# Attention scores of three sequences in two single-pass parts, rows to the operand tile by way of DRAM, and a new instruction order

## The reference, cut to what matters

```python
x = x + _L0_attn_ref(_layernorm(x), ...)  # "s": convolution, then a scan over 512 steps of 256 x 16 states
x = x + _L0_ffn_ref(_layernorm(x), ...)   # "g": gated experts, 8 experts of which at most 2 count
x = x + _L1_attn_ref(_layernorm(x), ...)  # "t": attention, below
x = x + _L1_ffn_ref(_layernorm(x), ...)   # "f": ternary weights, 128 -> 512 -> 512 -> 512 -> 128
```

```python
def _L1_attn_ref(x, W_DQ, W_UQ, W_QR, W_DKV, W_UK, W_UV, W_KR, W_O):
    ...                                    # 16 heads, 8 plain and 4 rotated columns each
    Q = jnp.concatenate([Qc, Qr], axis=-1)
    K = jnp.concatenate([Kc, Kr], axis=-1)
    scores = jnp.einsum('bhqd,bhkd->bhqk', Q, K)
    scores = jnp.clip(scores, -80.0, 80.0)
    causal = jnp.tril(jnp.ones((S, S), dtype=bool))
    scores = jnp.where(causal, scores, -jnp.inf)
    weights = jax.nn.softmax(scores / jnp.sqrt(jnp.float32(d_qk)), axis=-1)
    attn = jnp.einsum('bhqk,bhkd->bhqd', weights, V)
```

## Time and profile before

| | before |
|---|---|
| time, median of 3 runs | 1694.17 us (1692.5 to 1697.28) |
| the profiled execution: its own time, its span | 1694.72 us, 1693.1 us |
| PE busy | 1541.0 us, 91% |
| DVE, ACT, POOL busy | 1393.5, 1257.4, 1136.6 us |

### The profile page before, as it was taken

How to read it: one execution, slowest core, us unless ns; L and a number is a source line. 1 busy time by engine, 2 the same in 40 slices (tenths; PEclk the granted TensorE clock), 3 DMA queues, 4 the chain that set the end, 5 groups by cost and what they waited for, 6 DMA issues and landing times. The chain is left out here.

```text
span 1693.1 us, 24277 instructions
## 1 busy us (share of the span) xinstructions
PE 1541.0 (91%) x7911; PEld 814.3 (48%) x7911; DVE 1393.5 (82%) x2695; ACT 1257.4 (74%) x2160; POOL 1136.6 (67%) x1019
## 2 busy tenths in 40 slices
PE   5446799999999999999999999999999799999997
PEld 2123344444444444444444434434444478788875
DVE  4899988999999999999999999997331677977773
ACT  4776788899898899989899898885656455555552
POOL 4996787878788887878888787885122255554442
PEclk9678799999999999999999999999999799999998
DMA  4000000000000000000000000002000000000000
GB/s 155 1 0 0 19 1 20 7 14 19 2 20 1 20 7 14 19 1 20 1 20 9 12 20 1 20 1 88 20 4 17 1 1 13 14 13 14 13 13 27
DMA packets 14689, 27.87 MB, mean 16 GB/s; under 512 B 3853, under 2 KB 4438, under 8 KB 14042
## 3 DMA queue, kind: packets, MB, share of 16 engines
q1 hardware_dynamic: 14554, 26.24, 5.4%
HBM read 9.46 MB, written 4.19 MB: 8 GB/s over the span
## 5 line engine op out<-in xcount | busy, mean ns | idle before, releaser
L615 POOL TENSOR_TENSOR sum_fast<-sum_fast,state_fast 128x512 f32<-128x512 f32 x448 | 578.0, 1290 | 74.1 <-DVE state_fast L597 41.0
L597 DVE TENSOR_TENSOR_SCAN state_fast<-state_fast,bank 128x512 f32<-128x512 f32 x512 | 597.9, 1199 | 8.8 <-ACT state_fast L582 7.9
L1007 ACT ACTIVATE prob_fast<-bank 128x1024 f32<-128x1024 f32 x320 | 325.0, 1017 | 117.4 <-PE bank L991 110.8
L991 PE MATMUL bank<-stacks_fast 64*128 64x512 f32 (+3 forms) x2048 | 363.6, 464 | 18.7 <-ACT prob_fast L1007 11.7
L582 ACT ACTIVATE state_fast<-chan_all_kept,neg_a_fast 128x512 f32<-128x512 f32 x512 | 349.7, 712 | 13.1 <-POOL sum_fast L615 7.4
L1051 POOL TENSOR_SCALAR_AFFINE_SELECT prob_fast<-prob_fast 128x512 f32<-128x512 f32 x256 | 165.6, 659 | 226.9 <-ACT prob_fast L1007 226.6
L991 PEld LDWEIGHTS bank<-stacks_fast 64*128 64x128 f32 x2048 | 171.6, 186 | 238.9 <-issue 101.1
L1643 POOL TENSOR_TENSOR cell_a_fast<-th_fast,cell_a_fast 128x512 fp32r<-128x512 f32 x64 | 90.1, 1408 | 154.9 <-ACT cell_a_fast L1518 154.9
L1068 PE MATMUL bank<-prob_fast,v_ext_fast 128*32 128x512 f32 (+3 forms) x2048 | 177.1, 441 | 15.9 <-POOL prob_fast L1051 8.1
L485 PE MATMUL bank<-xnt_s_fast,taps_fast 128*128 128x512 f32 (+3 forms) x256 | 129.7, 654 | 33.8 <-DVE chan_all_kept L540 22.8
L669 PE MATMUL bank<-resid_m_fast,xnt_g_fast 128*128 128x512 f32 x256 | 143.7, 646 | 10.4 <-DVE gate_fast L750 9.5
(11 more groups left out here) (205 smaller groups left out, 2497.5 us busy)
## 6 DMA issues: line engine op xcount, KB each, us to landing
stacks_fast<-parts_fast SPq DMA_DIRECT2D x128, 64.0 KB
stacks_fast<-rest_fast SPq DMA_DIRECT2D x128, 32.0 KB
out_x<-f_out_fast SPq DMA_DIRECT2D x16, 256.0 KB, 2.0
x_res_kept<-in_x SPq DMA_DIRECT2D x1, 2048.0 KB, 15.3
chan_all_kept<-in_h_t SPq DMA_DIRECT2D x2, 1024.0 KB, 7.3
x_res_kept<-in_x SPq DMA_DIRECT2D x1, 1024.0 KB, 10.9
chan_all_kept<-in_w_t SPq DMA_DIRECT2D x3, 256.0 KB, 2.9
x_res_kept<-in_x SPq DMA_DIRECT2D x2, 256.0 KB, 3.7
```

The source lines that it names most:

```text
L597: dve.tensor_tensor_scan(h[:], h[:], self.banks[0][:], 0.0, ALU.mult, ALU.add).then_inc(self.v_scan.sem)
L615: pool.tensor_tensor(total[:], total[:], h[:], ALU.add).then_inc(self.p_sum.sem)
L991: ins = pe.matmul(self.scores(b, step)[:, c:c + SEQ - P * kt], rows[:, 1, h // 2, P * kt:P * kt + P], rows[:, 0, h // 2, P * kt:SEQ], star ...
L1007: act.activation(self.probs[u % 2][:, i * 1024:(i + 1) * 1024], self.scores(b, 5 * g + n)[:], ACT.Exp, scale=SCALE).then_inc(self.a_prob.sem)
```

## The change

Line numbers in this section's rows of the new kernel are its own: L1055 is the score matmul (L991 before), L704 L669, L683 L648, L713 L678, L891 L854, L898 L859, L908 to L911 L869 to L872, L1132 L1068, L1139 L1075.

1. From sequence 13 on (`SPLIT = 13`), queries and keys are split into a part hi, rounded to the type fp32r, and the rest lo. hi and lo of a head's 12 rows stand below each other in `stacks`, keys as hi, lo, hi, lo and queries as hi, lo, lo, hi, so that 48 of the 64 rows hold all four products, and one matmul in fp32r takes the place of one in float32. ACT's copy rounds; DVE subtracts it from the PSUM bank (L965, 2 a sequence); POOL copies and subtracts the rotated rows (2 a sequence).
2. For every sequence, the rows go first to DRAM (`rows_q`, `rows_k`, two buffers each, taken in turn) and from there to `stacks`. Up to sequence 12 this takes 4 + 8 DMAs of 64 to 256 KB instead of 16 of 32 and 64 KB; from 13 on 10 + 16. `parts` and `rest0` are free when their rows are in DRAM, and no longer when `stacks` is written.
3. Small setup tiles share the room of `num`.
4. `TIMES` and `EDGES` are new: every engine's order in phase one changes.

```diff
-PERIOD, F_PERIOD = 70626, 24942
+PERIOD, F_PERIOD = 73747, 24942
...
-DMA_SIGNALS = {"stack_lo": 8, "stack_hi": 8}
+
+SPLIT = 13
+DMA_SIGNALS = {"out_rot": 2, "out_q": 1, "out_k": 1, "stack_lo": 4, "stack_hi": 4}
+DMA_SPLIT = {"out_rot_split": 5, "out_q_split": 3, "out_k_split": 2, "stack_lo_split": 8, "stack_hi_split": 8}
...
+        hi, lo = (self.rot_hi[:].bitcast(F32), self.rest[1]) if split else (self.rest[0], None)
+        for at, src in ((DH, hi), (DQK + DH, lo), (2 * DQK + DH, hi))[:3 if split else 1]:
+            sp.dma_start(q[s, at:at + DR].rearrange("d h p c -> (d h p) c"), src[0:NQ]).then_inc(out_rot.sem, 16)
...
+        for i, rows in enumerate((q, k)):
+            hi, lo = self.parts[:, i].bitcast(F32), self.parts_lo[:, i].bitcast(F32)
+            yield
+            sp.wait_ge(self.a_t_qk.sem, self.a_t_qk.at(b, i))
+            if split:
+                sp.wait_ge(self.v_t_lo.sem, self.v_t_lo.at(b - SPLIT, i))
+            for at, src in ((0, hi), (DQK, lo), (2 * DQK, hi))[:3 - i if split else 1]:
+                sp.dma_start(rows[s, at:at + DH].rearrange("d h p c -> (d h p) c"), src).then_inc(out_rows[i].sem, 16)
+        for half, name in enumerate(("stack_lo", "stack_hi")):
+            cols, moved = slice(half * PAIRS // 2, (half + 1) * PAIRS // 2), self.on_way(name, b)[0]
+            yield
             if b:
                 sp.wait_ge(self.t_score.sem, self.t_score.at(b - 1, 5 * GROUPS // 2 * (half + 1) - 1))
...
+            sp.wait_ge(out_rot.sem, self.on_way("out_rot", b)[1])
+            for i, rows in enumerate((q, k)):
+                sp.wait_ge(out_rows[i].sem, self.on_way("out_k" if i else "out_q", b)[1])
+                for parity in range(2):
+                    n = 2 * DQK if split else DQK
+                    for twice in range(2 if split else 1):
+                        r, at = 64 * parity + n * twice, 0 if i else DQK * twice
+                        sp.dma_start(stacks[r:r + n, i, cols].bitcast(F32),
+                                     rows[s, at:at + n, 2 * parity + half]).then_inc(moved.sem, 16)
...
         pe.wait_ge(self.a_t_sq.sem, self.a_t_sq.at(b, 1))
+        if b >= SPLIT:
+            pe.wait_ge(self.v_t_lo.sem, self.v_t_lo.at(b - SPLIT, 1))
...
+            dve.tensor_tensor(self.parts_lo[:, i], bank[:], parts[:, i].bitcast(F32), ALU.subtract).then_inc(self.v_t_lo.sem)
...
+        pool.tensor_copy(hi[:], full[:]).then_inc(done.sem)
+        pool.wait_ge(done.sem, done.at(b - SPLIT, 0))
+        pool.tensor_tensor(self.rest[1][:].bitcast(F32R), full[:], hi[:].bitcast(F32), ALU.subtract).then_inc(done.sem)
...
                     rows = stacks[64 * (h % 2):64 * (h % 2) + 64]
+                    rows = rows if b >= SPLIT else rows.bitcast(F32)
```

More of the change, by code:

```diff
@@ L886, in act_t_proj @@
             if b:
-                act.wait_ge(self.stack_lo.sem, self.stack_lo.at(b - 1, 7))
-                act.wait_ge(self.stack_hi.sem, self.stack_hi.at(b - 1, 7))
+                written, value = self.on_way("out_k" if i else "out_q", b - 1)
+                act.wait_ge(written.sem, value)
                 if i == 0 and not general:
                     act.wait_ge(self.t_t_norm.sem, self.t_t_norm.at(b - 1))
-            act.activation(parts[:, i], bank[:], ACT.Copy).then_inc(self.a_t_qk.sem)
+            act.activation(parts[:, i] if b >= SPLIT else parts[:, i].bitcast(F32), bank[:], ACT.Copy).then_inc(self.a_t_qk.sem)
             act.activation(self.squares[:, i], bank[:], ACT.Square).then_inc(self.a_t_sq.sem)
@@ L979, in pe_scores @@
                 if n == 0 and g % 2 == 0:
-                    moved = self.stack_hi if g else self.stack_lo
-                    pe.wait_ge(moved.sem, moved.at(b, 7))
+                    moved, value = self.on_way("stack_hi" if g else "stack_lo", b)
+                    pe.wait_ge(moved.sem, value)
                 step = 5 * g + n
@@ L1149, in act_t_setup @@
         act.wait_ge(self.t_fold_t.sem, self.t_fold_t.at(0, 0))
-        act.activation(self.lat_t[:], bank[0:2 * LAT, 0:DM], ACT.Copy)
+        act.activation(self.lat_t, bank[0:2 * LAT, 0:DM], ACT.Copy)
         for swap in range(2):
@@ L1227, in pe_t_setup @@
         pe.wait_ge(self.v_center.sem, self.v_center.at())
-        pe.matmul(bank[0:2 * LAT, 0:DM], self.lat_w[:], self.center[:], start=True, stop=True)
-        pe.matmul(bank[:, DM:DM + 2 * DR], self.center[:], self.kr_w[:], start=True, stop=True).then_inc(self.t_fold_t.sem)
+        pe.matmul(bank[0:2 * LAT, 0:DM], self.lat_w, self.center[:], start=True, stop=True)
+        pe.matmul(bank[:, DM:DM + 2 * DR], self.center[:], self.kr_w, start=True, stop=True).then_inc(self.t_fold_t.sem)
         yield
@@ L1242, in pool_setup @@
         pool.memset(self.eps[:], EPS).then_inc(self.p_eps.sem)
-        pool.memset(self.stacks[:], 0.0).then_inc(self.p_stacks.sem)
+        pool.memset(self.stacks[:].bitcast(F32), 0.0).then_inc(self.p_stacks.sem)
         for v in self.v_ext:
@@ L1814 @@
     t["out"] = nc.dram_tensor("out_x", (P, NSEQ * NT, DM), F32, kind="ExternalOutput").ap()
+    t["rows_q"] = nc.dram_tensor("rows_q", (2, 3 * DQK, 4, PAIRS // 2, SEQ), F32, kind="Internal").ap()
+    t["rows_k"] = nc.dram_tensor("rows_k", (2, 2 * DQK, 4, PAIRS // 2, SEQ), F32, kind="Internal").ap()
     build(nc, t)
```

272 lines of the change are left out of this document (148 added, 124 removed).

## The result

The changed kernel takes 1707.94 us, median of 4 runs (1706.2 to 1710.92), against 1694.54 for the kernel before on the same chip. The ratio is 1.0077, 95% interval 1.0063 to 1.0091: slower by 0.8%. I had forecast 1677, faster, with 1653 to 1695 as the range. The profiled execution has a span of 1709.4 us.

What follows compares the result with a forecast made beforehand. PE and DVE were taken to bound the middle, PE alone the stretch behind the last scan. 1172.1 + 48.9 + 43.1 + 4.5 + 22.5 + 9.3 = 1300.4 against 1317.9, 17.5 less, so 1677 us from 1694.2; range 1653 to 1695.

Steps and rivals of the forecast that it cites:

- The five marks of my sum: End of phase one: 13's scores at 1172.1, windows 48.9, 43.1, 4.5 waiting, 22.5 and 9.3 to the end: 1300.4.
- The price of a score step: Score matmuls from sequence 13 on: 0.40 us in fp32r against 1.06 in float32, 39.6 us saved over three sequences.
- I put the new order's effect on the middle at zero: Sequences 0 to 12: periods stay at 73.5 us, the longer DMA hop hidden behind 17 us of PE rows.
- the rival of the winning middle: The new order also fills PE's 1.9 us idle a period, up to 21 us: 1652 to 1668, chance 0.23.
- The slower rival, the gate in the middle: PE waits at L713 for the gate each period, 11 to 12 us per us lost; 1704 at 2.5; chance 0.13.
- y comes at about 1162: Behind the last scans: the last y at about 1162, PE waiting from 1153, scores of 13 at 1172.
- Sequences 13 and 14: Windows between first scores: 13 falls from 64.1 to 48.9 us, 14 from 56.5 to 43.1, the gate of 15 costing 3.
- The rows' way: Sequence 15's keys by DRAM to stacks: 13.0 us from the keys' start, PE waiting 4.5 us for the DMA.
- The rows' path makes the time: Rival: slow loads of 192 KB into stacks make each of three sequences wait 5 us more: 1692, chance 0.08.
- The clock: Rival: PE's clock falls to 0.5 in the last 32 us, costing 12 us: 1689, chance 0.11.
- one of my signs of being wrong: Signs: periods differing by 0.5 us or more, a PE wait at L713 in each, or clock 0.5 before 1290.

Runs made afterwards that it cites:

- the best: Changed kernel with twelve parts of sequences 12 to 15 moved and the projection making the keys' rotated rows 16 times (64 partitions): 1675.2 us, ratio 0.9889.
- the kernels with twelve and thirteen moves: Changed kernel with twelve or thirteen parts of sequences 12 to 15 moved in the engines' order: 1700.9 us with twelve, 1708.6 with thirteen.
- the old order: Changed kernel, split and way by DRAM kept, with the order tables of the kernel before: 1804.8 us, ratio 1.0657.
- the last four kernels: Changed kernel with rows from 64 partitions, 1703.0 us; with twelve moves, 1700.9; with both, 1675.2; with both and all scores in float32, 1700.1.
- the order without the way: Changed kernel with twelve parts of sequences 12 to 15 moved, the slow rows' way kept: 1700.9 us, ratio 1.0034.
- the way without the order: Changed kernel where the projection makes the keys' rotated rows 16 times, so DMAs read 64 partitions, nothing moved: 1703.0 us, ratio 1.0048.

## Why the prediction was wrong

The five marks of my sum against the trace: the last scan 1152.9 (measured 1137.5), scores of 13 at 1172.1 (1169.3), then 48.9 (65.8), 43.1 and 4.5 (62.4), and 31.8 to the end (37.2). So -15.4 to the last scan, +12.6 from there to the scores, +16.9, +14.8 and +5.4: 34.3 in all, 1334.7 for 1300.4. Of the 14.8, 2.0 are a slip of mine in adding: 56.5 - 13.2 - 2.8 + 1.6 + 3 is 45.1 and not 43.1, and the forecast should have read 1679.

Two steps made the forecast wrong: the waits behind the last scan, which I took over from the kernel before, and the price of the rows' way.

**The price of a score step was right** (0.43 us for 0.40). But 0.40 was a choice between bounds, and the weight loads that I worked it out from don't show: at full clock, steps of four matmuls take 0.44 us and steps of two 0.43. What it is worth wasn't: of 39.6 us, 15.8 in the changed kernel and 25 in the best (18 by its profiled execution). I had taken it off two windows as if PE stayed their limit. PE's work did go away; idle time and half clock stepped in.

**The middle**: "I put the new order's effect on the middle at zero" failed in my favour. It gives 1.0 us a period, as in the rival of the winning middle, which I gave 0.23. The slower rival, the gate in the middle, did not happen.

**"y comes at about 1162"**, 9 us behind the last scan: it came 17 behind (1154.6, where L683 starts), since POOL stood 4.7 us in front of sequence 13's rotated rows with the last scans' sums queued behind them. I had counted DVE's rows there and not POOL's.

**Sequences 13 and 14**: I counted what moved on PE and took over the waits of before. The order and the split's pieces made new ones. PE's values can't start before their shared bank has been read: in the new order they stand right behind the keys and wait 2.2 us for ACT's squares even without the split, and 2.9 with the subtraction of the low part (twice). A mask stood behind POOL's sum and split of the rotated rows (4.4; without the split the longest wait for a mask is 3.1); the gate of 15 was late by 3.7, with the split or without, where I had 3. Each is a reader of a bank or a row in an in-order queue that the diff and the new order show.

**The rows' way was mis-sized, and that decided.** "Two issues out 1.4, four of queries in 2.8 ... and some 0.3 for 192 KB instead of 64", 13.0 us from the keys' start: in the changed kernel it took sequence 15 21.3 (L891 at 1276.2, scores at 1297.5), and 28.6 from the first row out. I costed issues and landings and not bytes: 1.9 MB out, of it 0.26 MB at 25 GB/s, and 3.1 MB in at 172. The wait of 4.2 us that I found "right" in the trace (4.5 forecast) was right by accident: PE itself came late. "The rows' path makes the time" was among my rivals with 0.08 and 5 us a sequence; uncovered, a wait is 6 to 14 us in the kernels with twelve and thirteen moves and up to 21.7 in the old order. That this is a cause rests on the last four kernels: the order without the way gives 7 us, the way without the order 5, both together 33. Each of the two long chains covered the other. How the 34.3 us divide between the two isn't shown.

**The clock** I priced as a rival for the last 32 us alone (0.11). It fell at ten places from 1076 to the end of the run-out, in float32 sequences too; clock 0.5 before 1290 was one of my signs of being wrong. Of 197 us 54 ran at half clock, with PE busy for 42.6 of them; that work takes half as long at full clock, so up to 21 us, more than the whole loss of 13. It is an upper bound: work that ends sooner may only wait longer.

That the best kernel stands at 1675.2, beside my 1677, doesn't make the forecast right: it has a period 1.0 us shorter, and a way for the rows that the change didn't have.

## What to carry to other kernels

Cost a DMA by bytes, by how many partitions it touches, and by what is queued behind it on the issuing queue; issue and landing times read from small transfers say nothing of it. When an operation is added that reads a shared buffer, find who writes that buffer next, on every engine, before looking at its own duration. And when undoing one suspected wait gains nothing, look what is waited for in its place before dropping the theory: two chains that cover each other show their price only when both are shortened.
